# Expert sums by accumulating gathers, with the weight applied in the copy out of PSUM

## What is computed

```python
probs = jax.nn.softmax(logits, axis=-1)
topk_w, topk_idx = jax.lax.top_k(probs, TOP_K)                 # 4 of 32 experts
topk_w = topk_w / jnp.sum(topk_w, axis=-1, keepdims=True)
combine = jnp.sum(jax.nn.one_hot(topk_idx, E, dtype=x.dtype) * topk_w[..., None], axis=1)
act = jax.nn.silu(g) * u                                       # per expert, 96 wide
eo = jnp.einsum('tei,eih->teh', act, w_down)
routed = jnp.einsum('te,teh->th', combine, eo)
return (routed + sh).reshape(orig_shape)                       # sh: shared expert, gated
```

## Time and profile before

| | us |
|---|---|
| median of 3 runs (lowest to highest) | 486.38 (485.72 to 487.09) |
| the profiled execution | 485.03 |
| its span, first to last instruction | 483.3 |
| PE busy | 386.3 (80%) |
| DVE busy | 329.7 (68%) |
| POOL busy | 292.6 (61%) |
| ACT busy | 260.1 (54%) |

### The profile page before, as it was taken

The page is one execution under the profiler, slowest core; times in us unless marked ns, Lnnn a source line. Parts: engine busy times, 40 slices in busy tenths (PEclk is TensorE's granted clock), DMA queues, the critical chain, the costliest instruction groups (busy, mean ns, idle before and its releaser), DMA issues.

```text
span 483.3 us, 8882 instructions
## 1 busy us (share of the span) xinstructions
PE 386.3 (80%) x2576; PEld 343.2 (71%) x2576; DVE 329.7 (68%) x1150; ACT 260.1 (54%) x495; POOL 292.6 (61%) x336
## 2 busy tenths in 40 slices
PE   0765898852299999995999999768888798898895
PEld 0754787641188889884999999757777686777774
DVE  5889787869245566550138778757898989884633
ACT  1250134300056666652566776567668677668673
POOL 4998777777777777773777777267777770000000
PEclk9996998976589999996899999989999999999999
DMA  7899991111335656645376666321322220100010
GB/s 188 280 356 284 344 373 55 52 49 46 121 122 187 212 189 198 198 159 170 116 226 206 205 205 212 105 71 50 97 74 77 73 75 25 43 24 22 24 34 22
DMA packets 48205, 67.26 MB, mean 139 GB/s; under 512 B 8841, under 2 KB 25634, under 8 KB 48162
## 3 DMA queue, kind: packets, MB, share of 16 engines
q1 hardware_dynamic: 39970, 49.93, 31.8%
q0 software_dynamic: 8192, 16.79, 11.6%
HBM read 28.93 MB, written 35.65 MB: 134 GB/s over the span
## 4 chain that ended last, share of the span: by engine, by line
POOL 32%; DVE 22%; PE 20%; issue 14%; ACT 7%; DMA 3%; SPq 1%; DVEq 0%; ACTq 0%; POOLq 0%
POOL slot_rows L563 13%; POOL onehot L577 6%; PE ps L752 6%; POOL route_tmp L577 6%; DVE trig L1333 3%; PE ps L743 2%; ACT L1105 2%; PE ps L865 2%; DVE mx L1467 2%; PE ps L727 2%; POOL tab_tmp L517 2%; POOL trig L517 1%; DVE rows L1484 1%; PE ps L898 1%; PE ps L735 1%
## 5 line engine op out<-in xcount | busy, mean ns | idle before, releaser
L563 POOL DMA_INDIRECT slot_rows<-xn_tok,slot_of x128 | 135.6, 1059 | 39.5 <-issue 39.5
L577 POOL DMA_INDIRECT onehot<-expert_rows,slot_of x64 | 61.8, 965 | 37.8 <-issue 18.9
L1317 DVE TENSOR_TENSOR act<-sg,ps 128x384 f32<-128x384 f32 x48 | 26.6, 554 | 81.3 <-ACT sg L977 80.9
L577 POOL DMA_INDIRECT route_tmp<-expert_rows,slot_of x64 | 62.3, 973 | 19.5 <-issue 19.5
L743 PE MATMUL ps<-w_dn,actT 96*128 x384 | 51.0, 275 | 1.5 <-ACT actT L995 1.5
L743 PEld LDWEIGHTS ps<-w_dn,actT 96*128 96x128 f32 x384 | 46.8, 192 | 2.1 <-issue 2.0
L977 ACT ACTIVATE sg<-ps 128x384 f32<-128x384 f32 x48 | 23.6, 491 | 38.5 <-PE ps L752 38.2
L727 PE MATMUL ps<-ident,rows 128*128 128x128 f32 x192 | 32.1, 293 | 12.1 <-DMA rows<-slot_rows 10.5
L752 PE MATMUL ps<-w_gu,raw_fc 128*128 x192 | 37.8, 343 | 0.0
L727 PEld LDWEIGHTS ps<-ident,rows 128*128 128x128 f32 x192 | 23.7, 149 | 18.7 <-DMA rows<-slot_rows 15.3
L986 ACT COPY zeros<-ps 128x512 f32<-128x512 f32 x48 | 28.2, 587 | 15.6 <-PE ps L743 15.2
(11 more groups left out here) (225 smaller groups left out, 899.5 us busy)
## 6 DMA issues: line engine op xcount, KB each, us to landing
slot_rows<-zeros SPq DMA_DIRECT2D x12, 1024.0 KB, 9.4
rows<-slot_rows SPq DMA_DIRECT2D x48, 256.0 KB, 3.2
expert_rows<-zeros SPq DMA_DIRECT2D x48, 256.0 KB, 2.5
x_tok<-in_L_attn_x_dram SPq DMA_DIRECT2D x8, 256.0 KB, 5.2
slot_rows<-xn_tok,slot_of POOLq DMA_INDIRECT x128
hs_t<-xn_tok SPq DMA_DIRECT2D x16, 128.0 KB, 2.1
out_dram<-raw_fc SPq DMA_DIRECT2D x16, 128.0 KB, 1.8
w_dn<-in_L_ffn_w_down_dram SPq DMA_DIRECT2D x1, 1536.0 KB, 15.1
```

Source lines behind the costliest of these rows:

```text
L563: g.indirect_dma_start(out=slot_rows[r], out_offset=bass.IndirectOffsetOnAxis(ap=slot_of[:, n:n + 1], axis=0), in_=xn_tok[:, r * HT + t, : ...
L577: g.indirect_dma_start(out=gath[b % 4][:, j, :], out_offset=None, in_=expert_rows[r], in_offset=bass.IndirectOffsetOnAxis(ap=slot_of[:, n: ...
L1317: v.tensor_tensor(act[u][:].rearrange("p (a b) i -> p a b i", a=2), sg[u][:].rearrange("p (a b) i -> p a b i", a=2), ps[:, 1 + 2 * u:3 + 2 ...
```

## The change

`slot_rows` gets wider rows: 136 numbers (544 bytes) instead of 128 (512 bytes), of which four are the token's weights and four its expert numbers. They stand beside the normalized row in SBUF, so that the same scatter takes them along. `expert_of` holds the expert of each slot tile, now on all partitions.

In each group DVE works out the weight of each slot (`row_weights`): it compares the row's four expert numbers with the tile's expert, multiplies by the four weights and adds up. That is three small instructions, ahead of `hidden`. The copy out of PSUM multiplies by this weight: in the first half ACT does it in four instructions of 128 x 128, in the second half DVE does it in one of 128 x 512, after its other work of the stage and before `row_weights` and `hidden`. A load also waits for `row_weights` of the group whose buffer it takes.

The gathers get `compute_op=ALU.add` and go straight into `sh_tok`: for each pair of sequences 16 gathers, over four tiles j in turn for each k, each waiting until the one before it into the same tile has landed. `sum_step` and `sum_experts`, the four gather buffers and the wait on `c_f` are gone; `silu_f` and `tanh_f` wait for the gathers themselves.

```diff
+RW = P + 8
...
+        sent_rows = sb("sent_rows", [P, NT, RW])
+        xn_tok = sent_rows[:, :, 0:P]
+        top_w = sent_rows[:, :, P:P + TOP0]
+        top_e = sent_rows[:, :, P + TOP0:RW]
...
                     sp.wait_ge(e_xT, r * SG + it - 4 + 1)
+                    sp.wait_ge(e_row_w, r * SG + it - 4 + 1)
...
-                if b >= 4:
-                    pool.wait_ge(c_f, b - 3)
-                for j in range(2 * TOP0):
-                    n = b * 2 * TOP0 + j
-                    g.indirect_dma_start(
-                        out=gath[b % 4][:, j, :], out_offset=None, in_=expert_rows[r],
-                        in_offset=bass.IndirectOffsetOnAxis(ap=slot_of[:, n:n + 1], axis=0)).then_inc(g_in[b % 4], 16)
+                for k in range(TOP0):
+                    for j in range(GT):
+                        n = (p * GT + j) * TOP0 + k
+                        if p or k:
+                            pool.wait_ge(g_in[j], 16 * (p * TOP0 + k))
+                        g.indirect_dma_start(
+                            out=sh_tok[:, p * GT + j, :], out_offset=None, in_=expert_rows[r],
+                            in_offset=bass.IndirectOffsetOnAxis(ap=slot_of[:, n:n + 1], axis=0),
+                            compute_op=ALU.add).then_inc(g_in[j], 16)
...
-                a.copy(eo[slot], bank(6)).then_inc(e_out, 1)
+                sc.wait_ge(e_row_w, n + 1)
+                for j in range(GT):
+                    last = a.activation(eo[slot][:, j * P:(j + 1) * P], ps[:, 6, j * P:(j + 1) * P], ACT.Identity,
+                                        scale=row_w[slot][:, j:j + 1])
+                last.then_inc(e_out, 1)
...
+            def row_weights(n):
+
+                slot = n % 4
+                if n:
+                    dve.wait_ge(e_row_w, n)
+                dve.wait_ge(rows_in[slot], 16 * (n // 4 + 1))
+                link(v.tensor_tensor(picks[:], rows[slot][:, :, P + TOP0:RW],
+                                     expert_of[:, n * GT:(n + 1) * GT].rearrange("p (j a) -> p j a", a=1)
+                                     .to_broadcast([P, GT, TOP0]), ALU.is_equal))
+                link(v.tensor_tensor(picks[:], picks[:], rows[slot][:, :, P:P + TOP0], ALU.mult))
+                if n >= 4:
+                    dve.wait_ge(e_out, n - 3)
+                v.tensor_reduce(row_w[slot][:], picks[:], AX.X, ALU.add).then_inc(e_row_w, 1)
+
+            def copy_out(n):
+
+                slot = n % 4
+                dve.wait_ge(e_dn, n + 1)
+                dve.wait_ge(e_row_w, n + 1)
+                dve.wait_ge(e_stored[slot], n // 4 * 16)
+                v.tensor_tensor(eo[slot].rearrange("p (j d) -> p j d", d=P), ps[:, 6, :].rearrange("p (j d) -> p j d", d=P),
+                                row_w[slot][:].rearrange("p (j a) -> p j a", a=1).to_broadcast([P, GT, P]),
+                                ALU.mult).then_inc(e_out, 1)
...
-                if step == 1:
-                    sum_experts(2 * q)
-                if step == 2:
-                    sum_experts(2 * q + 1)
                 if step == 3:
                     mix(q, False)
                     stats1(q)
                 if step == 4:
                     rstd1()
+                if n >= SG and not half_starts(n):
+                    copy_out(n - 1)
                 if n + 1 < N:
+                    row_weights(n + 1)
                     hidden(n + 1, (n + 1) % 2)
+            copy_out(N - 1)
...
                 if turned(b) is not None:
-                    rstd1(summed(b))
-                elif summed(b) is not None:
-                    sum_experts(summed(b))
+                    rstd1()
```

More of the change, by code:

```diff
@@ L83, in turned @@
     return NORM_AT.get(b)
-def summed(b):
-    for ahead in (2, 1):
-        if b >= 0 and turned(b + ahead) is not None:
-            return 2 * turned(b + ahead) + 2 - ahead
-    return None
 def gated(b):
@@ L221, in build @@
         rec = sb("rec", [P, 2, SEQ])
-        rows_4 = sb("rows_4", [P, 4, GT * P])
-        rows = [rows_4[:, u, :] for u in range(4)]
+        rows_4 = sb("rows_4", [P, 4 * GT * RW])
+        rows = [rows_4[:, u * GT * RW:(u + 1) * GT * RW].rearrange("p (j d) -> p j d", d=RW) for u in range(4)]
+        picks = sb("picks", [P, GT, TOP0])
+        row_w = [sb(f"row_w{u}", [P, GT]) for u in range(4)]
         eo = [zeros[:, u * GT * P:(u + 1) * GT * P] for u in range(4)]
@@ L242, in build @@
         f_act = out_cs[:].rearrange("p c (a d) -> p (c a) d", d=P)
-        f_w = [sb(f"f_w{u}", [P, 2 * TOP0]) for u in range(2)]
         st1 = sb("st1", [P, 4, 6])
@@ L330, in build @@
         e_stored = [sem(f"e_stored{u}") for u in range(4)]
-        g_in = [sem(f"g_in{u}") for u in range(4)]
+        e_row_w = sem("e_row_w")
+        g_in = [sem(f"g_in{j}") for j in range(GT)]
         xr_in = [sem(f"xr_in{u}") for u in range(2)]
-        c_f = sem("c_f")
+        c_mixed = sem("c_mixed")
         c_fact = sem("c_fact")
@@ L613, in tile_ids @@
                 pe.wait_ge(ex_ready, r + 1)
-                pe.transpose(ps[0:1, 7, 0:ST], tile_ex[0:ST, :], ident[0:ST, 0:ST]).then_inc(exT_row, 1)
+                pe.matmul(ps[:, 7, 0:ST], ones[0:ST, :], expert_diag[:], start=True, stop=True).then_inc(exT_row, 1)
             def turn_half(r):
@@ L995, in copy_aT, with summed_up @@
                 a.copy(actT[u][:], ps[0:I0, 5, :]).then_inc(e_aTs, 1)
+            def summed_up(p):
+                for j in range(GT):
+                    sc.wait_ge(g_in[j], 16 * TOP0 * (p + 1))
+                if p:
+                    sc.wait_ge(c_mixed, p)
             def silu_f(p):
-                sc.wait_ge(c_f, 2 * p + 2)
-                a.activation(f_act, f_sb, ACT.Silu).then_inc(c_fact, 1)
+                summed_up(p)
+                a.activation(f_act, sh_tok[:, p * GT:(p + 1) * GT, :], ACT.Silu).then_inc(c_fact, 1)
             def copy_xn(p):
@@ L1025, in stage_e @@
                     copy_xT(n + 2, n % 2)
-                if not half_starts(n):
+                if not half_starts(n) and n < SG:
                     copy_out(n - 1, (n - 1) % 4, (n - 1) // 4)
@@ L1124, in _ @@
             link = chain.link
[L1125 removed]
+            v.memset(zeros[:, 0:GT * RW], 0.0).then_inc(zero_set, 1)
             def row_stats(t):
@@ L1353, in mix @@
                 if tanh:
-                    link(v.scalar_tensor_tensor(out=f_sb, in0=f_act, scalar=1.0, in1=f_sb, op0=ALU.add, op1=ALU.mult))
+                    for j in range(GT):
+                        dve.wait_ge(g_in[j], 16 * TOP0 * (p + 1))
+                    link(v.scalar_tensor_tensor(out=f_sb, in0=f_act, scalar=1.0, in1=sh_tok[:, p * GT:(p + 1) * GT, :],
+                                                op0=ALU.add, op1=ALU.mult))
                 dve.wait_ge(s_tok, NSEQ)
@@ L1422, in make_gates @@
                     v.tensor_tensor(pa[:, :, 2, :], ga, pa[:, :, 1, :], ALU.subtract).then_inc(d_gate, 1)
+            row_weights(0)
             hidden(0, 0)
```

81 lines of the change are left out of this document (32 added, 49 removed).

## The result

| | median, us | runs | span of the profiled run, us | clock |
|---|---|---|---|---|
| before, beside it | 486.74 | 485.72 to 489.81 (4) | 483.3 (the run of the rows) | 0.938 |
| changed | 549.86 | 548.10 to 550.86 (4) | 546.3 | 0.894 |

The ratio is 1.131 [1.127, 1.135]: slower by 63 us, where +15.4 was forecast and 522 was the upper end of the range. The profiled executions differ by the same 63.0.

The account below looks back on a forecast made before the run. The chain that ended last named POOL for 32% of the span, DVE 22%, PE 20%. Terms -4.5 + 0 + 4.5 + 12 + 1 + 2.4 = +15.4 us gave 502 us, range 487 to 522.

Parts of the forecast that it names:

- The adding gathers: POOL's gathers into sh_tok: even a doubled landing of 4.1 us fits the 5.1 between dependent gathers, so cost 0.
- Its room: Experts' second half: 14 us of slack remain over 64 gathers, so each may take up to 1.50 us.
- adding gathers issue slowly: Rival: POOL's part of a gather half as long again, 1.73 us each, giving 532 us; chance 0.14.
- Attention: Attention stage: eight sums on DVE go, gaining 4.5 us (bounds 2 and 8).
- Scatter side: POOL's scatters: rows 6% longer, but issue sets the pace, so 0 (bounds -1 and +3).
- First half: Experts' first half: row_weights on DVE delays hidden and four ACT copies delay loads, +4.5 us (bounds 1 and 9).
- Second half: Experts' second half: copy_out and row_weights on DVE delay hidden and the loads, +12 us (bounds 5 and 18).
- steps 3 and 4: Stages of the second half's five-stage turn where DVE's added work does not fit: +1.3 and +1.2 us.
- the term of the late loads: Second half: step 4's late copy_out delays the load behind it, making act_T two stages on late by +1.3 us.
- End: End of the experts' stage: the last copies on DVE delay attention's start by +2.4 us (1 to 4).
- Loads: Row loads in the experts' stage: doubled gather traffic lengthens them a little, +1 us (0 to 4).

Follow-up runs that it names:

- e10: The changed kernel without its 128 adding gathers and the waits for them: 620.03 us.
- e12: The changed kernel without its gathers, and without two of the three small row_weights instructions on DVE: 616.79 us.
- e9: The kernel before without its 128 gathers and the waits for them: 608.04 us.
- e15: The kernel before with useless POOL memsets, 128x480 ahead of each scatter and 128x584 ahead of each plain gather: 600.44 us, ratio 0.815.
- e2: The kernel before with only the add put into its gathers, nothing else of the change: 674.75 us, ratio 0.919.
- e13: The kernel before with a useless POOL memset of 128x480 ahead of each scatter and each gather: 589.37 us, ratio 0.791.
- e18: The kernel before with useless POOL memsets, 128x256 ahead of scatters and 128x96 ahead of gathers: 532.26 us, ratio 1.088.
- e3: The changed kernel with adding gathers that take 64 instead of 128 numbers of a row: 675.15 us, ratio 0.919.
- e7: The changed kernel itself, run again on the chips of the follow-up runs: 674.88 us, ratio 0.922.
- e1: The changed kernel with plain gathers, the add left out, so no sum is formed: 770.57 us, ratio 1.051.
- e6: The changed kernel with plain gathers instead of adding ones, repeated on another chip: 771.21 us, ratio 1.049.
- e17: The kernel before with useless POOL memsets of 128x256 ahead of scatters and gathers alike: 543.71 us, ratio 1.112.

## Why the prediction was wrong

**The step that failed** is "The adding gathers": "The trace has none. Nearest row: a plain gather", costed at 0. The step watched the wrong part of a gather. It asked whether the landing would double and serialise the chain of four, and found room, rightly: the landing went from 2.52 to 3.19, and POOL never waited for it. The Trainium skill's figure ("DMA: Bandwidth & Descriptors", Anatomy of one DMA) is about 2 us fixed for a DMA. The estimate of 5 us made from it there is above the 3.19 measured. What the sum left at nothing, and only a rival had, is what POOL pays to start one. With the add a gather makes 144 packets instead of 32 and keeps POOL busy for 1.55 us instead of 0.97; 128 gathers, each 0.58 us further from the one before, are 74 us of POOL.

**Its room was nearly right, which is why the miss can be priced.** The step put the point from which gathers bind at 1.50 us. By stages measured without gathers, attention of the changed kernel would start at 313.4 + 4.3 + 8.9 + 2.3 = 328.9; it starts at 355.55, 7.4 after the last landing at 348.14, so 26.6 too late over 63 gathers, and by this estimate binding starts at 1.857 - 0.42 = 1.43. Attention binds from about 1.5, by the table. The rival "adding gathers issue slowly" had this mechanism, place and point, and gave 532 for a POOL part half as long again, 1.73 apart. With the measured 1.85 its own sum is 502 + 64 x 0.35 + 16 + 64 x 0.12 = 548; measured 549.86. That it comes so near is in part luck: the experts' half lost 26.6 where this sum has 22.4, attention 25.8 (190.75 against 165.0 without gathers) where it has 23.7, and the rest of the span is 494 by stages where the forecast has 498.7. What was wrong with the rival is its size and above all its chance, 0.14. Against it stood that scatter and gather cost POOL nearly the same, so direction doesn't matter. But both are plain, so that row said nothing of an adding one.

**The other terms**, point by point:

- *Attention* -4.5: without gathers 170.7 to 165.0, so -5.7; inside the bounds.
- *Scatter side* 0: L561's mean is 1076 against 1059, but the first half's last scatter, which the experts wait for, starts at 124.39 against 126.48; no cost is seen. The second half's comes at 217.99 against 215.48, before POOL's first gather in both.
- *First half* +4.5: its intervals sum to 84.7 against 80.4, +4.3, and in e10 a pair of stages is 0.36 longer, eleven of which are 4.0. Four copies take 1.14 (forecast 1.15) and stay hidden; `row_weights` is the part that shows, since e12 with a third of it is back at 6.99 a pair. In the changed kernel:

```profile
157.14 0.17 DVE L1346 TENSOR_TENSOR picks<-rows,expert_of 128x16 f32<-128x16 f32 x1
157.35 0.18 DVE L1349 TENSOR_TENSOR picks<-picks,rows 128x16 f32<-128x16 f32 x1
157.56 0.17 DVE L1352 TENSOR_REDUCE row_w<-picks 128x4 f32<-128x16 f32 x1
157.64 0.55 DVE L1334 TENSOR_TENSOR act<-sg,ps 128x384 f32<-128x384 f32 x1
158.11 0.42 DVE L1308 TENSOR_TENSOR rec<-rec 128x256 f32<-128x256 f32 x1
158.17 1.14 ACT L990 ACTIVATE zeros<-ps,row_w 128x128 f32<-128x128 f32 x4 [0.31 <-PE ps L745]
```

  The row of before had 0.16 us of idle time ahead of the same product; here there is none.
- *Second half* +12: +8.9 in e10. The place is right (steps 3 and 4), the wait is another: PE's matmuls wait 7.4 us for `copy_out` on DVE and 1.0 for `hidden`. They wait 3.5 for rows where e9 has 0.2, so the term of the late loads is seen too.
- *End* +2.4: 6.69 - 4.37 = 2.3.
- *Loads* +1 by doubled traffic: rows land in 3.2 us in both; not seen.

Together, without the gathers, +9.8 by stages and +12.0 by the medians, where 14.4 was forecast. With binding gathers most of it vanishes. POOL waits for the first half's +4.3, but the second half's +8.9 and the end lie beside its gathers: between first and 65th gather e15 and e2, which have neither, take 129.6 and 130.8 us and the changed kernel 130.4. So the 63 us are 3.5 of the first half and 59.5 of POOL's gathers, and in the 59.5 the missing sums are already taken off (3.3 us against e15, 6.4 against e2).

## What to carry to other kernels

An indirect DMA has two prices: its landing, and what the issuing engine pays to start it. Where that engine sends a long row of them back to back, the second one decides, and any new feature of the transfer (an add above all) must be priced there, or the forecast must give the unseen price a real chance. Padding the issuing engine by a known amount of useless work, as e13 to e18 do, measures from which price it binds without building the change. And work that is saved on an engine with room (eight sums on DVE, 5.7 us) can't pay for work added on the one that sets the end (128 x 0.58 on POOL).

## What the runs showed of the hardware

- A gather of 128 rows that adds in memory keeps POOL busy for 1.55 us instead of 0.97, makes 144 packets instead of 32, and lands 3.2 us after its start instead of 2.5. With rows of half the size POOL's time and the packets are the same (e2, e3, e7).
- On four chips the same kernel takes 734 to 745 us instead of 486 to 489, since PE, ACT and DVE stop together, each for up to 48 us at a time (e1, e6), while POOL starts indirect DMAs 1.28 us apart. Spaced 1.74 to 1.77 apart by useless memsets the pauses go, and the kernel takes 589. With gathers at 1.57 and scatters at 1.77 it takes 565, the best found there; it would be slower than the kernel before on a chip without the pauses (e17: 544 against 489), so no version beats both kernels on both kinds of chip. What the engines wait for, what makes the chips differ, and where between 1.28 and 1.57 the limit for gathers lies, is open.
- Four ACT instructions of 128x128 with a per-partition weight, read from PSUM, take 1.14 us together, and one of 128x512 takes 0.59.
